# Second attention and FP4 feed-forward: two quotient buffers, weights turned in the attention's front, masks and scales with a second tensor, and the first tile's prologue split

## What is computed

```python
def fp4_quant_dequant(x):
    xb = x.reshape(shape[:-1] + (shape[-1] // BLOCK, BLOCK))
    scale = jnp.maximum(jnp.max(jnp.abs(xb), axis=-1, keepdims=True) / 6.0, 1e-12)
    idx = jnp.searchsorted(_MID, jnp.abs(xb / scale))
    return (_GRID[idx] * jnp.sign(xb) * scale).reshape(shape)
gate = fp4_linear(x, w_gate)
h = jax.nn.silu(gate) * fp4_linear(x, w_up)
return fp4_linear(h, w_down)
```

## Time and profile before

| what | us |
|---|---|
| median of 3 runs (lowest, highest) | 1002.08 (996.93, 1007.6) |
| the profiled execution | 1005.61 |
| its span, first to last instruction | 1003.8 |
| mean granted TensorE clock, share of full | 0.951 |
| TensorE matmul busy | 898.1 (89%) |
| VectorE, ScalarE, GpSimd busy | 626.4, 437.4, 304.1 |

### The profile page before, as it was taken

The page is one execution under the profiler, slowest core; times in us unless marked ns, Lnnn a source line. Parts: engine busy times, 40 slices in busy tenths (PEclk is TensorE's granted clock), DMA queues, the critical chain, the costliest instruction groups (busy, mean ns, idle before and its releaser), DMA issues.

```text
span 1003.8 us, 19829 instructions
## 1 busy us (share of the span) xinstructions
PE 898.1 (89%) x7228; PEld 685.1 (68%) x7228; DVE 626.4 (62%) x1317; ACT 437.4 (44%) x946; POOL 304.1 (30%) x311
## 2 busy tenths in 40 slices
PE   2997799999997978999999967799999996699996
PEld 1764687878876747878888844587878874366664
DVE  3455577878854594545545465566777764678872
ACT  0442466666664561111111112466666675345442
POOL 8003466767782260000000004000000001476673
PEclk9998799999998798999999977999999999999998
DMA  9788644444333469121111204345565500000000
GB/s 258 219 238 203 113 93 92 93 93 93 62 106 98 138 214 250 46 67 32 32 32 48 65 3 82 74 85 112 107 117 109 106 27 21 0 11 16 16 10 22
DMA packets 98157, 90.45 MB, mean 90 GB/s; under 512 B 43554, under 2 KB 85410, under 8 KB 97954
## 3 DMA queue, kind: packets, MB, share of 16 engines
q1 hardware_dynamic: 98066, 89.25, 36.6%
HBM read 69.36 MB, written 19.63 MB: 89 GB/s over the span
## 4 chain that ended last, share of the span: by engine, by line
PE 72%; DVE 12%; DMA 5%; POOL 3%; ACT 3%; issue 2%; SPq 2%; DVEq 0%; POOLq 0%; ACTq 0%
PE ps L988 13%; PE ps L805 8%; PE ps L859 8%; PE ps L791 8%; PE ps L994 7%; PE ps L819 7%; PE ps L1062 3%; DMA Qz<-mT 3%; PE ps L709 3%; PE ps L1078 2%; PE ps L868 2%; POOL Pr L645 2%; PE ps L779 2%; PE ps L828 1%; DMA X<-x_in 1%
## 5 line engine op out<-in xcount | busy, mean ns | idle before, releaser
L1444 DVE TENSOR_REDUCE ext<-ps 112x2 f32<-112x750 f32 x256 | 232.6, 933 | 66.5 <-PE ps L791 63.4
L1175 ACT ACTIVATE Pr<-ps 125x448 f32<-125x448 f32 x384 | 199.2, 542 | 88.5 <-PE ps L805 75.0
L805 PE MATMUL ps<-Qz,Kp 98*125 98x224 f16 x768 | 130.7, 265 | 14.0 <-DMA Qz<-mT 11.7
L791 PE MATMUL ps<-Kp,Qz 96*112 96x375 f16 x512 | 122.6, 332 | 5.8 <-DMA Qz<-qscr 4.9
L805 PEld LDWEIGHTS ps<-Qz,Kp 98*125 98x125 f16 x768 | 94.8, 137 | 47.2 <-DMA Qz<-mT 15.9
L859 PE MATMUL ps<-wv,ctx 128*125 128x256 f32 x384 | 120.7, 400 | 1.9 <-DVE xT L1417 1.0
L599 POOL TENSOR_TENSOR X<-X,bo 112x256 f32 x32 | 22.5, 724 | 284.6 <-DVE Pr L1362 233.0
L1585 DVE TENSOR_TENSOR Pr<-Pr,ps 128x336 f32<-128x336 f32 (+2 forms) x86 | 32.7, 381 | 88.9 <-ACT Pr L1257 73.8
L819 PE MATMUL ps<-Pr,Vx 125*32 125x112 f32 x3072 | 86.9, 261 | 0.0
L819 PEld LDWEIGHTS ps<-Pr,Vx 125*32 125x32 f32 x3072 | 71.4, 110 | 14.9 <-ACT Pr L1175 10.3
L1589 DVE SCALAR_TENSOR_TENSOR X<-ps,W,X 112x256 f32<-112x256 f32 x167 | 70.7, 477 | 17.3 <-PE ps L994 17.3
(11 more groups left out here) (176 smaller groups left out, 1417.1 us busy)
## 6 DMA issues: line engine op xcount, KB each, us to landing
ctx<-ctxT SPq DMA_DIRECT2D x56, 375.0 KB, 3.7
Kp<-kscr SPq DMA_DIRECT2D x96, 187.5 KB, 4.8
kscr<-ksp SPq DMA_DIRECT2D x24, 375.0 KB, 4.2
Pr<-wexp SPq DMA_DIRECT2D x20, 384.0 KB, 4.2
Qz<-qscr SPq DMA_DIRECT2D x174, 28.0 KB, 4.1
expert<-wexp SPq DMA_DIRECT2D x12, 384.0 KB, 3.9
Pr<-ctxT SPq DMA_DIRECT2D x8, 375.0 KB, 4.5
kscr<-Pr SPq DMA_DIRECT2D x8, 375.0 KB, 3.9
```

The source lines that it names most:

```text
L791: last = mm(ps[0:S, 2 * (p % 2) + u, 0:M], Qz[0:96, q0 + u * S:q0 + (u + 1) * S], Kp[0:96, k0:k0 + M], start=True, stop=True)
L805: last = mm(ps[0:KC, 4 + k % 2, u * 2 * S:(u + 1) * 2 * S], Kp[0:98, k0:k0 + KC], Qz[0:98, q0:q0 + 2 * S], start=True, stop=True)
L1175: A(Pr[g % 2][0:KC, j, GI * t:GI * t + GI, :].rearrange("r h q -> r (h q)"), ps[0:KC, 4 + k % 2, 0:GI * S], ACT.Exp, scale=scale).then_inc ...
L1444: V.tensor_reduce(ext[0:S, 2 * p:2 * p + 2], ps[0:S, 2 * (p % 2):2 * (p % 2) + 2, 0:M], AX_X, red).then_inc(row_maximum_taken, 1)
```

## The change

- h's quotient and step have two buffers each (`qrh[par]`, `qch[par]`). GpSimd's pass is now x_back(i+2), x_over(i+3), h_over(i+1), h_back(i); VectorE's is h_exponents(i), x_exponents(i+2), x_scales(i+3), ffn_sum(i-2), x_round(i+2), gate_h(i+1), h_round(i). TensorE's and ScalarE's passes keep their order.
- The masks of the exponents and the scales' lower bound take a constant tensor as a second input (`exponent_bits`, `floor_of_scales`, two memsets at the start) in place of an immediate.
- The twelve turns of the weights go into the second attention's front: seven ahead of the first group's turn, five between its projection and the second group's turn. They use PSUM banks 6 and 7 and land in buffers that are free then. The third of the down weights' groups is cut otherwise; there still are four.
- `tile_norms` of the first ten tiles (12 before), x_scales(0), x_exponents(0) and, on ScalarE, x_magic(0) stand ahead of the last batch's normalise and values_turned; x_round(0) and x_scales(1) stand behind the last residual. The other four tiles' statistics stand behind the first pass.

```diff
+FIRST = 10
...
-PE_FRONT = "turn project turn project turn R R project R R turn R R project R R M V V V V W W"
+PE_FRONT = "weight weight weight weight weight weight weight turn project weight weight weight weight weight turn project turn R R project R R turn R R project R R M V V V V W W"
+ACT_FRONT = "weight weight weight weight weight weight weight turned high weight weight weight weight weight turned high turned high turned high"
...
-          for c0, c1 in ((0, 2), (2, 4), (4, 5), (5, 6))]
+          for c0, c1 in ((0, 2), (2, 3), (3, 5), (5, 6))]
...
-        qrx, qcx = (spare1[:, at + D * n:at + D * (n + 1)] for n in range(2))
-        fgT, fuT = (spare[:, C2 * FI * n:C2 * FI * (n + 1)].rearrange("p (c o) -> p c o", c=C2) for n in (0, 1))
-        fdT = spare[:, 2 * C2 * FI:2 * C2 * FI + 6 * D].rearrange("p (c o) -> p c o", c=6)
+        xT2f = xT2[:, :, :].rearrange("p c n -> p (c n)")
+        qrh, qch = ([spare1[:, at + FI * n:at + FI * (n + 1)], xT2f[:, 3 * D + FI * n:3 * D + FI * (n + 1)]] for n in (0, 1))
+        qrx, qcx, xq = (xT2f[:, D * n:D * (n + 1)] for n in range(3))
+        fgT = [own_expert[2 + c][:, 0:FI] for c in range(C2)]
+        fuT = [kspf[c][:, 0:FI] for c in range(C2)]
+        fdT = [own_expert[c // 3][:, D * (c % 3):D * (c % 3 + 1)] for c in range(6)]
+        qrw, qcw, qtw = (xT2[:, 0, 16 * NW16 * n:16 * NW16 * (n + 1)] for n in range(3))
...
+            nc.gpsimd.memset(floor_of_scales[:, :], 1e-12).then_inc(constants_set, 1)
+            nc.gpsimd.memset(exponent_bits[:, :], 0x7F800000).then_inc(constants_set, 1)
...
-            def h_over(i):
+            def h_over(i, par):
                 pool.wait_ge(h_scales_ready, i + 1)
-                wait_from(pool, hq_ready, i)
-                over(qrh, hf, rch, NH, h_divided)
+                if not isinstance(i, int) or i >= 2:
+                    pool.wait_ge(hq_ready, i - 1)
+                over(qrh[par], hf, rch, NH, h_divided)
 
             def h_back(i, par):
                 pool.wait_ge(h_rounded, i + 1)
-                G.tensor_tensor(qrh, qrh, qch, ALU.subtract).then_inc(h_less_magic, 1)
+                G.tensor_tensor(qrh[par], qrh[par], qch[par], ALU.subtract).then_inc(h_less_magic, 1)
                 pool.wait_ge(h_less_magic, i + 1)
                 wait_from(pool, hq_is_turned, i)
-                over(qh, qrh, sch[par], NH, hq_ready)
+                over(qh, qrh[par], sch[par], NH, hq_ready)
 
             def ffn_batch(i, par, left=3):
-                h_over(i)
                 if left >= 2:
                     x_back(i + 2, par)
                 if left >= 3:
                     x_over(i + 3)
+                if left >= 1:
+                    h_over(i + 1, 1 - par)
                 h_back(i, par)
 
             x_over(0)
             x_over(1)
             x_back(1, 1)
             x_over(2)
+            h_over(0, 0)
...
+                def turn_weights(k):
+
+                    if k == 0:
+                        pe.wait_ge(weights_quantised, B)
+                    if k >= 2:
+                        pe.wait_ge(weights_copied, k - 1)
+                    w, pieces = TURNS[k]
+                    for a, c, col in pieces:
+                        if w < 2:
+                            src, r, n = fq[0:FCH[a], (6 * w + a) * D + 128 * c:(6 * w + a) * D + 128 * c + 128], 128, FCH[a]
+                        else:
+                            at = 12 * D + a * FI + 128 * c
+                            src, r, n = fq[:, at:at + FCH[c]], FCH[c], 128
+                        last = nc.tensor.transpose(ps[0:r, 6 + k % 2, col:col + n], src, ident[0:n, 0:n])
+                    last.then_inc(weights_turned, 1)
 
                 def turn_group(q):
...
+                    if q == 1:
+                        pe.wait_ge(weights_copied, len(TURNS))
...
+                    weights, turned, high = iter(range(len(TURNS))), iter(range(NG)), iter(range(NG))
+                    for step in ACT_FRONT.split():
+                        if step == "weight":
+                            weights_out(next(weights))
+                        elif step == "turned":
+                            q = next(turned)
+                            t = 4 if q else 0
+                            act.wait_ge(group_turned, q + 1)
+                            A(xTs[q], ps[:, t:t + 2, 0:QG * S], ACT.Copy).then_inc(group_xT_copied, 1)
+                        elif step == "high":
+                            q = next(high)
+                            act.wait_ge(group_projected, q + 1)
+                            for m in range(C2):
+                                last = A(qsps[:, q, :, m, 0, :], ps[:, (6 if q else 2) + m, 0:QG * S].rearrange(
+                                    "p (b q) -> p b q", q=S), ACT.Identity, bias=bqk[1][:, m:m + 1])
+                            last.then_inc(group_high_ready, 1)
 
...
+                if l == 1:
+                    x_magic(0)
...
+                ch.link(V.scalar_tensor_tensor(sc[:, :], am[:, :], 1.0 / 6.0, floor_of_scales[0:sc.shape[0], 0:nb],
+                                               ALU.mult, ALU.max))
...
+                V.tensor_tensor(c.bitcast(U32), r.bitcast(U32), exponent_bits[0:c.shape[0], 0:n],
+                                ALU.bitwise_and).then_inc(done, 1)
...
+            def ffn_batch(i, par, left=3, sums=True):
+
+                h_exponents(i, par)
+                if left >= 2:
+                    x_exponents(i + 2)
+                if left >= 3:
+                    x_scales(i + 3, 1 - par)
+                if sums:
+                    ffn_sum(i - 2)
+                if left >= 2:
+                    x_round(i + 2)
+                if left >= 1:
+                    gate_h(i + 1, 1 - par)
+                h_round(i, par)
+
+            dve.wait_ge(constants_set, 6)
...
+                if l == 1:
+                    tile_norms(0, FIRST)
+                    x_scales(0, 0)
+                    x_exponents(0)
                 normalise(g0 + B - 1)
                 residual(g0 + B - 1, B - 1)
+                if l == 1:
+                    x_round(0)
+                    x_scales(1, 1)
                 if l == 0:
...
-            def ffn_batch(i, par, left=3, sums=True):
-
-                if left >= 2:
-                    x_exponents(i + 2)
-                if sums:
-                    ffn_sum(i - 2)
-                h_exponents(i)
-                if left >= 3:
-                    x_scales(i + 3, 1 - par)
-                if left >= 2:
-                    x_round(i + 2)
-                h_round(i)
-                if left >= 1:
-                    gate_h(i + 1, 1 - par)
-
-            FIRST = T - 2
-            for t in range(FIRST):
-                if LAST_OF[t] > B - 5:
-                    tile_stats(t)
-            tile_norms(0, FIRST)
-            x_scales(0, 0)
-            x_exponents(0)
-            x_round(0)
-            x_scales(1, 1)
             x_exponents(1)
             x_round(1)
             x_scales(2, 0)
```

More of the change, by code:

```diff
@@ L883, in _ @@
                     values = iter([(j, c) for j in range(NJ) for c in range(C2)])
-                    turns, projects = iter(range(NG)), iter(range(NG))
+                    turns, projects, weights = iter(range(NG)), iter(range(NG)), iter(range(len(TURNS)))
                     for step in ((PE_FRONT if l else PE_FIRST) if b < 0 else PE_ORDER).split():
-                        if step == "turn":
+                        if step == "weight":
+                            turn_weights(next(weights))
+                        elif step == "turn":
                             turn_group(next(turns))
@@ L1322, in _ @@
             xq_turned(1)
-            ffn_batch(0, first=True)
-            with act.Fori(0, T - 3) as i:
-                ffn_batch(i + 1)
-            ffn_batch(T - 2, left=1)
-            ffn_batch(T - 1, left=0)
+            ffn_batch(0, 0, first=True)
+            with act.Fori(0, (T - 4) // 2) as i:
+                ffn_batch(i * 2 + 1, 1)
+                ffn_batch(i * 2 + 2, 0)
+            ffn_batch(T - 3, 1)
+            ffn_batch(T - 2, 0, left=1)
+            ffn_batch(T - 1, 1, left=0)
             h_turned(T - 1)
@@ new lines, in exponents, with add_magic, x_exponents @@
+            def exponents(r, c, done):
+                n = c.shape[1]
+                V.tensor_tensor(c.bitcast(U32), r.bitcast(U32), exponent_bits[0:c.shape[0], 0:n],
+                                ALU.bitwise_and).then_inc(done, 1)
+            def add_magic(r, c, done):
+                V.scalar_tensor_tensor(r, r, PRED, c, ALU.mult, ALU.add).then_inc(done, 1)
+            def x_exponents(i):
+                dve.wait_ge(x_divided, i + 1)
+                exponents(qrx, qcx, x_exponents_ready)
@@ new lines, in x_round, with h_exponents, h_round, gate_h @@
+            def x_round(i):
+                dve.wait_ge(x_magic_ready, i + 1)
+                add_magic(qrx, qcx, x_rounded)
+            def h_exponents(i, par):
```

(23 more changed lines are left out.)

154 lines of the change are left out of this document (59 added, 95 removed).

## The result

The changed kernel takes 1027.53 us (median of 4 runs, 1025.9 to 1030.62) beside 1002.21 us for the kernel before: ratio 1.0257 [1.0227, 1.0287], slower by 2.6%. The forecast was 1029 us, with a range of 1007 to 1043. The profiled execution has a span of 1026.3 us against 1003.8; that of before lay 3.4 above its median, so the spans differ by 22.5 and the medians by 25.3.

The account below looks back on a forecast made before the run. Bound by two loops side by side, TensorE's 8.8 us and one of 9.4 through VectorE, GpSimd and ScalarE; 28.3 + 3.0 - 4.3 - 4.8 + 4.4 = +26.6 gave 1032 profiled, 1029 us on the median, range 1007 to 1043.

Parts of the forecast that it names:

- Loop, +28.3: Steady feed-forward: twelve periods of 12.0 us plus 3.1 for the first tile's stall, against 118.9 before: 28.3 us slower.
- The walk from up(i) to up(i+1): Feed-forward: durations added from the end of up(i) through gate_h, h_round, h_over, GpSimd's work and turn_h: period 12.0 us.
- TensorE's ring: Feed-forward: up(i) leads through gate_h(i), h_over(i), h_back(i-1) and turn_h(i-1) to up(i+1) within one period, priced 12.0 us.
- the sum changes by 0.2: Feed-forward: if GpSimd's subtraction, not VectorE's h_exponents, goes first after h_over, the period changes by only 0.2 us.
- Stall of the first tile, 15.2: Feed-forward start: statistics for four tiles behind h_round(0) make gate_h(2) start some 15.2 us after up(1), not 12.1: +3.1.
- pass beside GpSimd: Feed-forward, a rival: the two-tensor masks and scales run beside GpSimd without taking turns; period 10.66, 1008 us, chance 0.2.
- Tail, +3.0: End of the feed-forward: about 24 us after up(13) instead of 21.0, so 3.0 slower; bounds 0 and +5.
- Seam, -4.3: Between last attention batch and feed-forward: gate(0) at 845.8 instead of 850.07, so 4.3 us faster; bounds 0 and -5.
- Front, -4.8: Front of the second attention: weight turns fill idle time and hold the clock, third projection 4.8 us earlier; bounds 0, -6.
- Clock in the loop, +4.4: Steady feed-forward: TensorE idles some 3 us per tile in one piece, losing the clock in two of twelve: +4.4 us.
- TensorE as the bound (980): Feed-forward, a rival: cutting the old loop leaves TensorE's own 8.8 us per tile; 980 us, chance 0.05.
- The clock in every second gap (1037): Feed-forward, a rival: the clock falls in every second of TensorE's gaps, adding 13.2 us; 1037 us, chance 0.15.

Follow-up runs that it names:

- run 1: Changed kernel with VectorE's and GpSimd's feed-forward passes in the order of before, all else as changed: 1000.39 us, ratio 0.9988.
- run 3: Changed kernel with TensorE's turn_h(i-1) behind up(i+1) and gate_h's scales waiting for h_back(i-2): 1026.74 us, ratio 1.0261.
- run 4: Changed kernel with ScalarE's h_magic(i) ahead of x_magic(i+2), TensorE as changed: 1032.15 us, ratio 1.0322.
- run 2: Changed kernel with the single-input masks and scales of before, nothing else undone: 1019.05 us, ratio 1.0202.
- run 9: The old loop with the seam undone too (first tile's norms, scales, mask and x_magic(0) behind the last residual): 999.46 us, ratio 0.9978.
- Run 11: The old loop with real matmuls, whose result nothing reads, added among the turns of the second attention's front: 992.74 us, ratio 0.9918.
- run 6: Changed kernel with only VectorE's pass in the order of before; GpSimd keeps h_over(i+1) ahead of h_back(i): 1026.84 us, ratio 1.0256.
- Run 10: The old loop with one swap on VectorE, x_round(i+2) ahead of x_scales(i+3): 987.49 us, ratio 0.9863.
- the old loop: Changed kernel with both passes' orders and the single-input masks and scales of before; front, seam and buffers stay: 996.2 us, ratio 0.996.

## Why the prediction came out, point by point

- **Loop, +28.3: measured +27.7.** The reordering as the cause is shown (run 1 takes all of it back). The walk from up(i) to up(i+1) gave 12.0, and the tile takes 11.84. But "ScalarE (x_magic, h_magic, silu) is done by about 11.1 [...] both have room, so nothing else sets the period" failed. I had VectorE win the port for both masks, each one ahead of GpSimd's instruction; GpSimd won both races, x's mask ended 0.28 behind the multiplication, and silu ended 12.25 after up and not 11.1. Cutting TensorE's ring (run 3) gave nothing, cutting ScalarE's led to the waits for up of run 4, cutting both gave 10.67. That 12.0 lies so near 11.84 is partly luck: "the sum changes by 0.2" was wrong too, for with GpSimd first TensorE's ring takes 11.52, 0.5 under the walk, and the ring that I left out is 0.3 longer than that.
- **Why GpSimd won the first race.** The walk let the subtraction start 0.08 behind h_over. The trace of before has that distance where a GpSimd instruction needs the last one's result (864.11 and 0.72, then 864.91); where it doesn't, the next starts 0.04 before the recorded end (866.21 and 0.62, then 866.79), and this subtraction doesn't need h_over's result. In the changed kernel it starts 0.04 before h_over's end (936.28), the mask 0.03 behind it.

```profile
864.11 0.72 POOL L655 TENSOR_TENSOR Pr<-Pr 128x256 f32<-128x256 f32 x1 [2.19 <-DVE Pr L1671]
...
864.91 1.15 POOL L645 TENSOR_TENSOR Pr<-Pr,scx 128x256 f32<-128x256 f32 x1
...
866.21 0.62 POOL L645 TENSOR_TENSOR Pr<-xn,rcx 128x256 f32<-128x256 f32 x1
...
866.79 1.67 POOL L667 TENSOR_TENSOR Pr<-Pr 128x704 f32<-128x704 f32 x1
```

- **Stall of the first tile, 15.2: measured 16.0**, with 1.8 of slow clock in it (up 4.37 against 2.53, after 4.06 idle), so without it somewhat shorter than worked out.
- **New forms beside GpSimd.** The rival "pass beside GpSimd" (1008) is refuted: 2.35 and 1.60. Taking turns as in the earlier trace rows was the right reading. It isn't special to two SBUF inputs: the old mask takes turns too (1.98, run 2). The Trainium skill, "GPSIMD Engine Reference", Key points, which counts VectorE instructions with two SBUF inputs among those that exclude GpSimd, agrees with this trace.
- **Tail, +3.0: measured +2.9.** turn_h(12) after 5.48 idle, down(12) 5.31 at half clock, as walked.
- **Seam, -4.3: measured -3.3** in the trace and by run 9. Mis-sized was what I left out: TensorE idled 4.77 ahead of turn_values, and the last project_out ran at 2.05 instead of 1.12. normalise itself was as late as worked out.
- **Front, -4.8: measured -2.6.** "Does a stretch of weight turns hold the clock? [...] So yes" failed. The granted clock went to 0.81 and 0.50 amid and behind the turns while TensorE never idled over 0.82 us up to turn_group's end, and the projections took 5.25 and 4.79. Run 11 kept everything and added matmuls in the gaps: 1.00 throughout, 3.27 and 3.27, 3.5 us. The Trainium skill, "TensorE: Matmul & The Clock Gate", PE-mode transpose, which I overruled with one window of 2 us at 846, was nearer: by its rule as I read it the projections keep 5.49 and 6.22. It isn't the whole account, since the second projection of run 1 ran at full clock behind the same turns. The added matmuls also close the gaps, so no run parts turns that don't count from gaps that do.
- **Clock in the loop, +4.4: measured 0** in the steady tiles (1.00 in 900:950). TensorE's idle time came in pieces (1.74 ahead of turn_h, 0.54 ahead of turn_xq) and not in one of 3. The clock does fall in other orders: behind 1.94 ahead of turn_h in run 4, behind 1.96 and 1.91 in run 6, behind 2.57 ahead of turn_xq in every second tile of run 3.
- **Rivals.** TensorE as the bound (980) was refuted for this order. Run 10 reaches that bound with another one, and the old loop's own order needed one swap for it. The clock in every second gap (1037) was refuted here. It is what happened in run 3, where it cost nothing, and what run 4 came close to, where it did.

The errors partly cancel, and that is luck: seam and front together were forecast 3.2 too good, the clock 4.4 too bad, and the 2.3 us that no edit accounts for stood in no term.

## What to carry to other kernels

Before an engine's pass is reordered, write down every ring that one period closes, through each engine's queue, with waits for a shared port in it; two rings within half a microsecond of each other hide one another: here cutting either alone gave nothing or a loss, and cutting both 12 us. A buffer more doesn't cut a ring which the order of two queues closes anew. Look first at what the engine that idles waits for, and what stands ahead of that in its queue: here one swap of x_round and x_scales was worth 8.7 us, and the two-buffer reordering cost 27.

## What the runs showed of the hardware

- Whether the clock holds depends on more than the length of one idle stretch. Ahead of turn_h, the changed kernel's 1.74 kept 1.00. In run 4 it fell behind 1.94, 2.05 and 2.71 and held behind 2.29 and 2.70. In run 6 it fell behind 1.91 and 1.96 and held behind 1.99 and 2.24. In run 3 every 2.57 ahead of turn_xq was followed by a down product of 4.74 instead of 3.05. What tells these apart stays open.
- The same stretch of weight turns lost the clock at different places. It starts at 585.7 in the changed kernel and the clock falls from 590 on; at 585.9 in the old loop, from 588 on; at 587.1 in the run without the seam (run 9), only at 594. The first projection of that run took 6.31, the slowest of all.
- A mask of 256 numbers a row takes 0.42 us alone (854.62 in the changed kernel) and 1.60 beside GpSimd's multiplication: the 1.32 that were left of the multiplication, and 0.28.
